# Adding the projection's bias with VectorE instead of TensorE in the last stage of a conv, attention and router block

## The reference

```
xn  = layernorm(x)
q,k,v = split(conv1d(xn, conv_w, width 3) + conv_b)        # 3 x 1024 columns
s   = block attention(q, k, v; blocks of 128, 16 heads) @ wo + bo
s   = s @ proj_w + proj_b                                  # 1024 -> 4096
w   = softmax(xn @ router_weight.T + router_bias), all but the top 8 of 64 set to 0
g   = silu(xn * sum(w) + w @ expert_bias)                  # 64 -> 4096
out = x + s * g
```

## Time and profile before

| what | value |
|---|---|
| time, median of 3 runs | 1060.77 us (1059.42 to 1061.2) |
| time of the profiled execution | 1059.76 us |
| span of its slowest core, which the trace shows | 1058.2 us (all cores 1055.0 to 1058.2) |
| busy: PE, DVE, ACT, POOL | 96%, 68%, 40%, 25% of the span |
| last stage, from the first matmul of piece 0 to the span's end | 920.8 to 1058.2 us |

### The profile page before, as it was taken

One profiled execution on the slowest core, in us unless ns is written; L12 is line 12 of the kernel. 1 busy time (PEld: TensorE's weight loads), 2 busy tenths in 40 slices (PEclk: granted clock), 3 DMA queues, 4 the chain that ended last, 5 costly groups with the idle time before them and its releaser, 6 DMA issues.

```text
span 1058.2 us, 16622 instructions; the slowest of 8 cores (1055.0 to 1058.2 us)
## 1 busy us (share of the span) xinstructions
PE 1010.7 (96%) x5314; PEld 475.7 (45%) x5314; DVE 715.6 (68%) x1057; ACT 427.3 (40%) x686; POOL 261.9 (25%) x327
## 2 busy tenths in 40 slices
PE   1778999999999999999999999999999999999997
PEld 1654544444444444444444444444444444433333
DVE  5897768767776256677776348787878754465555
ACT  3757634333332343333333255565556412044332
POOL 0774300001212111121221100011210100467765
PEclk9899999999999999999999999999999999999999
DMA  9944348789998798999989667768787889999884
GB/s 277 331 167 115 104 144 248 233 243 291 311 311 269 228 272 288 305 299 293 313 284 295 197 215 221 246 220 267 228 262 247 274 249 262 275 294 307 252 258 153
DMA packets 62857, 265.77 MB, mean 251 GB/s; under 512 B 7666, under 2 KB 7938, under 8 KB 60722
## 3 DMA queue, kind: packets, MB, share of 16 engines
q1 hardware_dynamic: 48340, 216.16, 63.6%
q0 software_dynamic: 14288, 48.44, 16.0%
q10 hardware_dynamic: 144, 0.12, 0.0%
HBM read 234.44 MB, written 30.43 MB: 250 GB/s over the span
## 4 chain that ended last, share of the span: by engine, by line
PE 87%; DVE 6%; issue 2%; DMA 2%; ACT 2%; DVEq 0%; SPq 0%; ACTq 0%
PE PS L220 85%; DVE AL L227 3%; DVE AL L269 2%; PE PS L224 2%; DMA AL<-x 1%; ACT AL L231 1%; DMA AL<-cw 1%; ACT PS L233 1%; DVEq L59 0%; DVE AL L1086 0%; SPq L73 0%; DVE tNm L786 0%; DVE tNmh L288 0%; DVE AL L978 0%; DVE tMv L276 0%
## 5 line engine op out<-in xcount | busy, mean ns | idle before, releaser
L220 PE MATMUL PS<-AL 128*128 128x512 bf16 (+4 forms) x4750 | 946.2, 367 | 4.3 <-ACT AL L231 3.3
L220 PEld LDWEIGHTS PS<-AL 128*128 128x128 bf16 (+3 forms) x4750 | 427.5, 102 | 511.2 <-issue 42.2
L227 DVE TENSOR_TENSOR AL<-AL 128x512 bf16<-128x512 f32 (+1 forms) x582 | 402.7, 720 | 145.8 <-PE PS L220 92.4
L231 ACT ACTIVATE AL<-AL 128x1024 bf16<-128x1024 f32 (+1 forms) x205 | 215.8, 1055 | 334.8 <-PE PS L220 294.3
L227 POOL TENSOR_TENSOR AL<-AL 128x512 bf16<-128x512 f32 (+1 forms) x83 | 126.6, 1536 | 75.8 <-ACT AL L231 43.7
L227 DVE TENSOR_TENSOR AL<-PS,AL 128x512 bf16<-128x512 f32 (+2 forms) x129 | 104.9, 814 | 38.8 <-PE PS L220 22.5
L231 ACT ACTIVATE AL<-PS 128x512 f32<-128x512 f32 (+2 forms) x88 | 55.9, 669 | 53.5 <-PE PS L220 27.6
L1086 DVE SCALAR_TENSOR_TENSOR AL<-AL,tSc,PS 128x1024 f32<-128x1024 f32 x32 | 41.0, 1280 | 52.1 <-PE PS L220 50.7
L231 ACT ACTIVATE AL<-AL,tScb 128x1024 f32<-128x1024 f32 (+1 forms) x33 | 37.0, 1124 | 82.1 <-DVE AL L1086 82.1
L224 PE MATMUL PS<-tCst,AL 128*128 128x128 f32 (+2 forms) x272 | 41.6, 298 | 25.7 <-DVE AL L227 9.8
L231 ACT ACTIVATE AL<-PS,tCst 128x512 bf16<-128x512 f32 (+1 forms) x56 | 36.5, 680 | 61.7 <-PE PS L220 61.6
(11 more groups left out here) (67 smaller groups left out, 255.1 us busy)
## 6 DMA issues: line engine op xcount, KB each, us to landing
AL<-cw SPq DMA_DIRECT2D x192, 768.0 KB, 6.6
AL<-x SPq DMA_DIRECT2D x16, 1024.0 KB, 29.9
AL<-x POOLq DMA_DIRECT2D x32, 512.0 KB, 7.3
out<-AL SPq DMA_DIRECT2D x31, 512.0 KB, 5.0
AL<-pw POOLq DMA_DIRECT2D x16, 512.0 KB, 8.4
AL<-pw SPq DMA_DIRECT2D x16, 512.0 KB, 7.6
wbs<-AL POOLq DMA_DIRECT2D x28, 256.0 KB, 7.7
AL<-wbs SPq DMA_DIRECT2D x24, 256.0 KB, 10.5
```

The costliest lines, as they stand in the source:

```text
L220: return PE.do(lambda e: e.matmul(out, lhsT, rhs, start=start, stop=stop, skip_group_check=skip), *toks, tok=tok)
L227: return eng.do(lambda e: e.tensor_tensor(out, a, b, op), *toks, tok=tok)
L231: return AC.do(lambda e: e.activation(out, in_, func, bias=bias, scale=scale), *toks, tok=tok)
```

## The change

- Last stage: the bias is no longer a product on PE. DVE adds it to the s banks in PSUM (1024 columns in place), from a copy that the host has spread over all 128 rows, ahead of its product with silu. The copy is loaded as 2 MB of float32 in two DMAs on SP's queue: `pbs` ahead of the `values` stage, `pb2` behind `wo_group`. In the last piece both adds and both products come first, then both sums with x.
- The expert biases are laid out on 128 partitions, the second half of each block of 1024 columns in partitions 64 to 127, and `router_pe2` makes a second copy of the weights there with 8 more matmuls. The two expert products of a piece so use different rows of PE.
- First stage: `vout(1)` is made by POOL in 10 of the 16 steps with `pt` below 2 (before 4); `prep(1)` moves from step 16, ahead of its sums, to the end of step 17; the first quarter of tile 3 is normalised in step 15 in place of 14.
- The preparation of the bias in two bf16 rows goes (one operation each on ACT and DVE, a memset of 4096 columns on DVE, five small DMAs), and so does the load of the ones.

```
@@ first stage
-                   12: [(6, 0)], 14: [(3, 0)], 15: [(7, 0)]}
+                   12: [(6, 0)], 15: [(3, 0), (7, 0)]}
...
                 if st_ == 16:
                     prep(0)
-                    prep(1)
...
-                if pt == 1 and i % 2 == 0:
+                if pt == 0 and i % 2 or pt == 1 and i % 4 != 3:
                     k_v0 = tt(GP, vout(1), E0, O1, ALU.add)
...
                 for j, what in applies.get(st_, ()):
                     apply(j, [what])
+                if st_ == 17:
+                    prep(1)
@@ router_pe2
-                dst = (pa, pb_)[j // 4][0:64, 128 * (j % 4):128 * (j % 4) + 128]
-                k = tr(dst, lgt3[:, j, :], t_i128f[:], rd["k"], tok=(j % 4 == 3))
+                for hh in range(2):
+                    dst = (pa, pb_)[j // 4][64 * hh:64 * hh + 64, 128 * (j % 4):128 * (j % 4) + 128]
+                    if hh == 0:
+                        tr(dst, lgt3[:, j, :], t_i128f[:], rd["k"])
+                    else:
+                        k = mm(dst, lgt3[:, j, :], t_i128f[:], True, True, tok=(j % 4 == 3), skip=True)
@@ loads
-        k_z = DV.do(lambda e: e.memset(pbhl, 0.0), k_unit23[7], tok=True)
...
+        k_pb = [SY.dma(S("sPB0"), pbs, d_pb[:, 0:2048].rearrange("p (g h f) -> p g h f", g=2, h=2),
+                       cv_tok[23], tb_free[0], a[NHB - 1]["t"], a[NHB - 1]["sp"]), None]
...
-        for i in range(4):
-            k_eb = staged(AC, ebv[:, 1024 * i:1024 * i + 1024], d_eb[:, 1024 * i:1024 * i + 1024])
+        for i in range(2):
+            k_eb = staged(AC, ebv[:, 1024 * i:1024 * i + 1024], d_eb[:, 1024 * i:1024 * i + 1024],
+                          k_unit23[7])
...
+        k_pb[1] = SY.dma(S("sPB1"), pb2, d_pb[:, 2048:4096].rearrange("p (j f) -> p j f", j=4), k_wope)
@@ finish
-                m_tok[m] = tt(DV, gw[i], bank2(4 * ((m + 1) % 2)), gw[i], ALU.mult, g_tok[m], s_tok[m])
+                b2 = bank2(4 * ((m + 1) % 2))
+                k = tt(DV, b2, b2, pbv[ci], ALU.add, s_tok[m], k_pb[ci // 2])
+                m_tok[m] = tt(DV, gw[i], b2, gw[i], ALU.mult, g_tok[m], k)
...
+                bs = [bank(4 * ((m + 1) % 2) + h) for h in range(2)]
+                ks = [tt(DV, bs[h], bs[h], pbv[ci][:, h, :], ALU.add, s_half[h]) for h in range(2)]
+                ks = [tt(DV, gw[i][:, h, :], bs[h], gw[i][:, h, :], ALU.mult, g_half[h], ks[h])
+                      for h in range(2)]
                 for h in range(2):
-                    k = tt(DV, gw[i][:, h, :], bank(4 * ((m + 1) % 2) + h), gw[i][:, h, :], ALU.mult,
-                           g_half[h], s_half[h])
-                    k = tt(DV, gw[i][:, h, :], gw[i][:, h, :], xg[i][:, h, :], ALU.add, k)
+                    k = tt(DV, gw[i][:, h, :], gw[i][:, h, :], xg[i][:, h, :], ALU.add, ks[h])
@@ last stage
             for h in range(2):
-                c0 = 1024 * ci + 512 * h
-                kg = mm(bank(sb0 + 2 + h), t_wmT[:, 128 * t:128 * t + 128], ebv[:, c0:c0 + 512],
-                        True, True, tok=(h == 1))
-                mm(bank(sb0 + h), t_ones[64:128, :], pbhl[:, c0:c0 + 512], True, False)
+                rows = slice(64 * h, 64 * h + 64)
+                kg = mm(bank(sb0 + 2 + h), t_wmT[rows, 128 * t:128 * t + 128],
+                        ebv[rows, 512 * ci:512 * ci + 512], True, True, tok=(h == 1))
```

More of the change, by code:

```diff
@@ L95, in build_program @@
     d_rw = din("rw", [128, 2048])
-    d_eb = din("eb", [64, D])
+    d_eb = din("eb", [128, 2048])
     d_cst = din("cst", [128, 233])
-    d_pb = din("pb", [32, 128])
+    d_pb = din("pb", [128, D])
     d_i128 = din("i128", [128, 128])
     d_mask4 = din("mask4", [128, 512])
-    d_ones = din("ones2", [64, 128])
     d_out = nc.dram_tensor("out", [8, 128, D], F32, kind="ExternalOutput").ap()
@@ L108, in build_program @@
     d_wb = dint("wbs", [28, 128, 1024])
-    d_pbs = nc.dram_tensor("pbs", [2, 32, 128], BF16, kind="Internal").ap()
     with contextlib.ExitStack() as es:
@@ L126, in build_program @@
         t_mask4 = sb("tMask4", [128, 512], BF16)
[L127 to L130, removed]
         t_mv = sb("tMv", [128, 18], F32)
@@ L138, in build_program @@
         t_scb = sb("tScb", [128, 8], F32)
-        t_wmT = sb("tWmT", [64, 1024], BF16)
+        t_wmT = sb("tWmT", [128, 1024], BF16)
         t_edge = sb("tEdge", [128, 192], F32)
@@ L194, in build_program @@
         qr = [bfv(B_QR + 1024 * i, 512).rearrange("p (q t) -> p q t", q=4) for i in range(2)]
-        ebv = bfv(B_U, D, 64)
-        pbhl = AL[64:128, B_U // 2:B_U // 2 + D]
+        ebv = bfv(B_U, 2048)
         stg = [f32v(B_F + 4096 * i, 1024) for i in range(4)]
@@ L577, in build_program @@
                     apply(j, [what])
+                if st_ == 17:
+                    prep(1)
                 if st_ == 20:
-                    for t, d in ((t_i128[:], d_i128), (t_mask4[:], d_mask4), (t_ones[64:128, :], d_ones)):
+                    for t, d in ((t_i128[:], d_i128), (t_mask4[:], d_mask4)):
                         k_c2 = GP.dma(S("sC2"), t, d)
-                    k_pbl = GP.dma(S("sC3"), t_pb[:], d_pb)
             if st_ != 16:
@@ L591, in build_program @@
         k_rt = rd["rt"]
[L593 to L596, removed]
         k_lgfree = DV.do(lambda e: e.tensor_scalar(lgT, p_lg, 2.0, t_rbT[:], ALU.mult, ALU.add),
@@ L661, in router_pe2 @@
                     rd["wm"] = DV.do(lambda e, h=h, b_=(pa, pb_)[h]: e.tensor_copy(
-                        t_wmT[:, 512 * h:512 * h + 512], b_[0:64, :]), k, tok=True)
+                        t_wmT[:, 512 * h:512 * h + 512], b_), k, tok=True)
             return rd["wm"]
@@ L922, in build_program @@
                 k_pwl[i] = SY.dma(S(f"sPW{i}"), pwb[i][kc], d_wb[8 * (i + 1) + kc], k_unit23[7])
-        for i in range(2):
-            k_pb = SY.dma(S("sPB2"), pbhl[i:i + 1, :],
-                          d_pbs[i].rearrange("(o a) b -> o (a b)", o=1), k_pbs, k_z)
+        pbs = f32v(B_TA, 2048).rearrange("p (g h f) -> p g h f", g=2, h=2)
+        k_pb = [SY.dma(S("sPB0"), pbs, d_pb[:, 0:2048].rearrange("p (g h f) -> p g h f", g=2, h=2),
+                       cv_tok[23], tb_free[0], a[NHB - 1]["t"], a[NHB - 1]["sp"]), None]
         PE.wait(a[NHB - 1]["nrm"], a[NHB - 1]["pts"], rd["wv"], rd["wv2"])
@@ L1014, in build_program @@
         k_wope = rd["wope"]
+        pb2 = vreg[:, 0:4, 0:4, :].rearrange("p j c f -> p j (c f)").bitcast(F32)
+        k_pb[1] = SY.dma(S("sPB1"), pb2, d_pb[:, 2048:4096].rearrange("p (j f) -> p j f", j=4), k_wope)
+        pbv = [pbs[:, 0], pbs[:, 1], pb2[:, 0:2, :], pb2[:, 2:4, :]]
         def load(m):
@@ L1061, in build_program @@
             load(m)
-        PE.wait(last["o"], a[7]["o"], *vfree[0], *vfree[1], k_eb, k_pb)
+        PE.wait(last["o"], a[7]["o"], *vfree[0], *vfree[1], k_eb, rd["wm"])
         DV.wait(last["pv"], rd["sc"])
@@ L1080, in build_program @@
                     s_tok[m] = mm(bank(sb0 + h), ao[kc][:, 128 * t:128 * t + 128],
-                                  pwb[ci][kc][:, 512 * h:512 * h + 512], False, kc == 7,
+                                  pwb[ci][kc][:, 512 * h:512 * h + 512], kc == 0, kc == 7,
                                   tok=(kc == 7))
@@ L1141, in _prep @@
         rw=cont(arr("L0_ffn_router_weight").reshape(64, 32, 128).transpose(2, 1, 0).reshape(128, 2048)),
-        eb=cont(arr("L0_ffn_expert_bias")),
+        eb=cont(arr("L0_ffn_expert_bias").reshape(64, 4, 2, 512).transpose(2, 0, 1, 3).reshape(128, 2048)),
         cst=cst,
-        pb=cont(arr("L0_attn_proj_b").reshape(32, 128)),
+        pb=cont(np.tile(arr("L0_attn_proj_b").reshape(1, D), (128, 1))),
         i128=np.eye(128, dtype=f32),
         mask4=cont(np.concatenate([m1] * 4, axis=1)),
-        ones2=cont(np.repeat((np.arange(64) < 2).astype(f32)[:, None], 128, axis=1)),
     )
```

## The result

The changed kernel takes 1075.35 us (median of 4 runs, 1071.97 to 1077.74) against 1060.45 us for the kernel before (median of 4 runs; the 1060.77 given ahead is that of 3 of them): ratio 1.0139, 95% interval 1.0108 to 1.017. It is slower, as forecast, but by 14.9 us in place of 6, and outside the range, which ended at 1071.5. The profiled execution took 1076.46 us, 16.7 more than that of before, and the spans differ by the same 16.7 us (1074.9 and 1058.2), both on core 7.

The account below looks back on a forecast made before the run. TensorE was taken to bound the kernel before, and a loop through VectorE the changed last stage. Loop +10.7, end +0.7, first stage -5.9 and router +0.4 made +5.9 us, so 1066.6 us; range 1060.5 to 1071.5.

Parts of the forecast that it names:

- first stage, up to about 145 us: First stage: sums taken off VectorE give 3.6 us and half of the moved `prep` 2.5; 5.9 us taken as gain.
- router_pe2: Router weights' second copy: eight more matmuls cost nothing beside the transposes, 1.0 us if behind; 0.4 us taken.
- the loop through VectorE: Last stage: piece start through z, add and product to next start takes 4.39, later 4.47 us, against 4.10; cost 10.7 us.
- the end: Last piece: VectorE's last operation ends about 7.16 us after the piece's start, against 6.46 before; cost 0.7 us.
- the signs by which the prediction called itself wrong: Piece starts 3.9 us apart, add well under 1.1, product under 1.2 after it, or step 17's transposes not 3 earlier.
- The rule weighed against the earlier trace: Last stage: semaphore chaining costs nothing, so add and product would be 0.2 us shorter; the prediction kept the trace's row instead.
- The wait that the prediction did price: Last stage, piece 1: ScalarE may wait some 3 us for the first weights; costed at nothing, once 3 us without cover.
- The sum's own upper bound: Whole kernel: first stage giving only 3 us, the loop costing 12.4 and the late cast give 1074 us.
- A time gained before 88 us arrives whole at the last stage: Between first and last stage: TensorE idles only 1.7 us in 832 from 88 to 920 us, so nothing is lost.
- the one that the first stage gives nothing: First stage: GpSimd or ScalarE's order becomes its bound; gain 0 to 2 us, time 1071 us; chance 0.1.
- the products not beside each other: Last stage: the two expert products don't run together, loop 0.23 us longer, 7 us in all, 1073 us; chance 0.04.
- the faster one, of a loop that doesn't close: Last stage: TensorE stays the bound; 1049 us at 3.87 us a piece, 1059 at 4.2; chance 0.1.

Follow-up runs that it names:

- Experiment 8: The changed kernel without the add in all pieces but the last, loads in the changed kernel's order: 1064.78 us, one run.
- experiment 4: The changed kernel with add and product of the previous piece ahead of z on VectorE in every piece: 1064.74 us, ratio 1.0024 to the kernel before.
- experiment 3: The changed kernel with `pb2` queued behind the first four loads of the last projection weights: 1072.03 us, ratio 1.0105 to the kernel before.
- experiment 6: As 5, but with `pb2` queued at piece 8 of the last stage: 1058.74 us, ratio 0.998 to the kernel before.
- experiment 2: The changed kernel with the router weights' second copy made by one DMA in place of eight matmuls: 1073.73 us, ratio 1.0114 to the kernel before.
- experiment 7: The changed kernel with `pb2` behind the four loads and add and product ahead of z, router copy still by matmuls: 1055.49 us, ratio 0.9966 to the kernel before.
- 5: The changed kernel with router copy by DMA, `pb2` behind the four loads, and add and product ahead of z: 1050.27 us, ratio 0.9902 to the kernel before.
- experiment 1: The kernel before with only the three edits of the first stage: 1056.67 us, ratio 0.9956 to the kernel before.

## Why the prediction was wrong

On core 7 the 16.7 us are made up so (each from the starts of the same matmuls in the two traces), beside what the prediction had:

| part | predicted | measured |
|---|---|---|
| first stage, up to about 145 us | -5.9 | -5.4 |
| `router_pe2` | +0.4 | +3.8 |
| on the way to the last stage | 0 | +1.1 |
| the loop through VectorE | +10.7 | +11.0 |
| late stores | 0 | +6.4 |
| the end | +0.7 | -0.2 |
| sum | +5.9 | +16.7 |

**The loop: right, step by step.** None of the signs by which the prediction called itself wrong came true, and every term stood within 0.02 us: start to z 0.50, z to add 1.20, add 1.23, gap 0.10, product and its end to the matmul 1.37; 4.40 and 4.47 in all, where 4.39 and 4.47 were predicted. (The 0.3 us over in the table are the one piece of 4.82.) The add with its output in PSUM, which no row of before showed, costs what the product costs. Experiment 8 shows that the add makes the loop, experiment 4 that its cost is its place in it and not VectorE's load. The rule weighed against the earlier trace rows (the Trainium skill, VectorE: DVE Perf Modes, The DRAIN you can't avoid), by which chaining with a semaphore costs nothing over chaining without, would have put the loop 0.2 us lower; this trace doesn't agree with it: add to product, with such a wait, is 1.33 us, z to add, without one for z, 1.20. (The stage's cost by that rule stands in the prediction once as 4.9 and once as 4.8; its working gives 4.8.)

**The loads: the step that failed.** The prediction costed `pb2` by who waits for it and for the four loads behind it: "a silu is needed only in the iteration after its own, some 3 us of cover". It asked what is late when these loads are late, and not what they do to everyone else's transfers. Four loads and `pb2`, 3 MB, were put into a stage that before already moved 1 MB per piece at a DMA share of 0.92 (930 to 1000 us); the backlog made stores late by 20 us, and a store has a reader eight pieces on, z. Moving the same loads ends the stalls in the profile (experiment 3) and moving 1 MB into the middle of the stage brings them back in every run (experiment 6). The sum had no term for it; on the slowest core it is 6.4 us of 16.7. No rival had it either. The wait that the prediction did price, ScalarE's for the first cast, came as said on the changed kernel, 3.6 us at most on any core, and lengthened no piece. But the late stores alone don't explain the miss: with them gone, experiment 3 still takes 1072.03 us, 5.4 above the forecast and 0.5 above the range. The rest is in the next two terms. (The sum's own upper bound was 1074; the range cut it off at 1071.5.)

**The router's copy: mis-sized.** The term was bounded by "nothing if they run beside them and 1.0 if behind". The pairs take 4.72 us where the transposes took 0.88, so the term is 3.8; by the starts of the last stage it is 2.9 (experiment 2) and 4.4 (experiment 7 against 5). The bound of 1.0 took a matmul of float32 for a transpose, and took for granted that alternating them costs nothing. The rows show the pair at 0.59 us where a transpose in a row of its kind took 0.11 to 0.13. What part is the matmul, which appears as two instructions, and what part the switching between them, was not separated.

**The first stage: right, but not all of it arrives.** It gave 5.4 us against 5.9. "A time gained before 88 us arrives whole at the last stage" failed for about 1 us: TensorE idles little in between because its loads come just in time, and once it is 5 us earlier some don't (experiment 1: 1.1 us more of idle time from 735 to 800 us).

**The end.** VectorE's last operations took 7.14 us from the last piece's start, as predicted (7.16); the last store landed sooner than before, which gave 0.9 back. Of the rivals, the one that the first stage gives nothing, and the products not beside each other, were wrong; the faster one, of a loop that doesn't close, became true in experiments 4, 5 and 7 only by changing the order.

## What to carry to other kernels

When an operation is added to an engine with idle time, write down the chain from the moment a buffer is taken to the moment it is given back; the same 1.2 us cost 0.3 us a piece inside that chain and nothing outside it, and putting the release ahead of the next piece's first operation took the kernel from 1.4% slower to 0.2% slower, and with the two other repairs to 1% faster. A transfer moved into a stage with a full DMA is priced by the slack of every other transfer there, those of its own queue above all, stores too, and by the slowest of eight cores. And a gain of TensorE in a stage fed just in time is worth a little less at the end than where it is made.

## What the runs showed of the hardware

- VectorE adds in place in PSUM, 1024 columns of float32, in 1.23 us, the same as its product with the output in SBUF.
- Two products of 64 rows each, on partitions 0 to 63 and 64 to 127 and into different banks, take the time of one (0.39 us for both).
- Eight pairs of a float32 transpose and a float32 matmul on different halves of the columns hold TensorE for 4.72 us, eight transposes alone for 0.88.
- A store of 512 KB took 5 to 11 us in the last stage before (core 7, medians of stretches of 15 us, DMA share up to 0.99), and up to 31 us with 3 MB of loads put beside it on the same queue, while x on the other queue took up to 17.
